# Self-attention's start: small loads issued by ScalarE, weight waits by block, the value weights' split moved

## What is computed

```python
x = _rmsnorm(tokens, norm_w)
q = x @ Wq
kv = x @ Wkv
k, v = jnp.split(kv, 2, axis=-1)
q = _head_rmsnorm(q, q_gamma)
k = _head_rmsnorm(k, k_gamma)
sim = jnp.einsum('bhid,bhjd->bhij', q, k)
sim = jnp.tanh(sim / SOFTCLAMP) * SOFTCLAMP
attn = jax.nn.softmax(sim * DIM_HEAD ** (-0.5), axis=-1)
out = jnp.einsum('bhij,bhjd->bhid', attn, v)
```

## Time and profile before

| | |
|---|---|
| median of 3 runs | 1844.41 us (1841.74 to 1845.32) |
| the profiled execution | 1844.2 us |
| its span (first to last instruction) | 1842.6 us |
| PE, DVE, ACT, POOL busy | 96%, 78%, 64%, 59% |
| granted TensorE clock, mean | 0.99 |

### The profile page before, as it was taken

One profiled execution on the slowest core, in us unless ns is written; L12 is line 12 of the kernel. 1 busy time (PEld: TensorE's weight loads), 2 busy tenths in 40 slices (PEclk: granted clock), 3 DMA queues, 4 the chain that ended last, 5 costly groups with the idle time before them and its releaser, 6 DMA issues.

```text
span 1842.6 us, 43008 instructions
## 1 busy us (share of the span) xinstructions
PE 1773.5 (96%) x14154; PEld 1481.7 (80%) x14154; DVE 1441.9 (78%) x3344; ACT 1170.6 (64%) x2674; POOL 1093.9 (59%) x1217
## 2 busy tenths in 40 slices
PE   5999999999997999999999999999999999989997
PEld 4777777777776899999999999899999999965443
DVE  5787789788887687777777788777777778788887
ACT  4876777765665466666566666656666656655664
POOL 3443445543344766866776755577878777552554
PEclk9999999999998999999999999999999999999999
DMA  4321323111113414414423433314322341551111
GB/s 157 109 74 64 117 75 111 41 50 30 40 50 104 156 48 149 129 60 133 129 91 105 142 104 94 110 48 120 93 73 82 93 113 47 129 118 50 57 62 63
DMA packets 109580, 166.89 MB, mean 91 GB/s; under 512 B 32488, under 2 KB 67672, under 8 KB 109512
## 3 DMA queue, kind: packets, MB, share of 16 engines
q1 hardware_dynamic: 91016, 129.77, 22.7%
q0 software_dynamic: 14656, 28.92, 5.7%
q10 hardware_dynamic: 3840, 7.34, 1.3%
HBM read 109.25 MB, written 50.46 MB: 87 GB/s over the span
## 4 chain that ended last, share of the span: by engine, by line
PE 58%; DVE 15%; issue 10%; POOL 7%; DMA 5%; ACT 4%; POOLq 1%; DVEq 0%; SPq 0%; ACTq 0%
PE att_ps_T L517 5%; PE att_ps_P L1648 5%; PE att_ps_SA L1672 4%; PE att_ps_P L1636 4%; PE att_ps_SB L579 4%; PE att_ps_P L1700 3%; PE att_ps_O L1636 3%; PE att_ps_T L1636 3%; PE att_ps_T L1648 2%; PE att_ps_P L1686 2%; DMA ca_ct<-ct_kept 2%; PE att_ps_O L1648 2%; PE att_ps_P L1711 2%; DMA out_dram<-ff_y_out 2%; PE att_ps_T L1700 2%
## 5 line engine op out<-in xcount | busy, mean ns | idle before, releaser
L1453 POOL TENSOR_TENSOR ca_pr<-ca_pr,ca_rec 112x750 f32<-112x750 f32 x256 | 366.8, 1453 | 182.8 <-DVE ca_rec L1932 179.8
L402 POOL TENSOR_TENSOR sa_p_lo<-sa_pr,sa_p_hi 112x448 fp32r<-112x448 f32 x128 | 147.2, 1162 | 255.2 <-ACT sa_p_hi L671 254.3
L1817 ACT ACTIVATE ca_big<-att_ps_P 126x384 fp32r<-126x384 f32 (+1 forms) x254 | 105.2, 449 | 65.1 <-PE att_ps_P L1686 63.1
L1811 ACT ACTIVATE ca_pr<-att_ps_SA,ca_nmax 112x750 f32<-112x750 f32 x128 | 113.7, 888 | 22.6 <-DVE ca_nmax L1928 12.2
L822 DVE RECIPROCAL sa_sums<-sa_sums 128x224 f32<-128x224 f32 x64 | 99.2, 1550 | 32.3 <-ACT sa_sums L680 31.8
L1937 DVE TENSOR_TENSOR ca_big<-att_ps_P,ca_big 126x384 fp32r<-126x384 f32 (+1 forms) x254 | 119.6, 498 | 5.5 <-ACT ca_big L1817 5.2
L1928 DVE TENSOR_REDUCE ca_nmax<-att_ps_SA 112x1 f32<-112x752 f32 x128 | 119.1, 930 | 0.1
L1928 DVE TENSOR_REDUCE ca_nmax<-att_ps_SB 112x1 f32<-112x752 f32 x128 | 119.0, 930 | 0.0
L1648 PE MATMUL att_ps_P<-ca_w_hi,ca_ct 128*126 128x256 f32 x570 | 116.5, 284 | 0.0
L1811 ACT ACTIVATE ca_pr<-att_ps_SB,ca_nmax 112x750 f32<-112x750 f32 x128 | 113.2, 885 | 0.1
L1686 PEld LDWEIGHTS att_ps_P<-att_ident,ca_pr 64*126 64x126 f32 (+1 forms) x1524 | 85.3, 138 | 13.7 <-issue 9.4
(11 more groups left out here) (344 smaller groups left out, 6659.1 us busy)
## 6 DMA issues: line engine op xcount, KB each, us to landing
ct_kept<-ca_ct SPq DMA_DIRECT2D x8, 1134.0 KB, 9.1
ca_ct<-ct_kept POOLq DMA_DIRECT2D x8, 1134.0 KB, 8.3
ct_kept<-ca_ct SPq DMA_DIRECT2D x8, 1116.0 KB, 11.5
ca_ct<-ct_kept POOLq DMA_DIRECT2D x8, 1116.0 KB, 10.4
sa_xin<-in_x_dram SPq DMA_DIRECT2D x16, 448.0 KB, 3.9
xt_kept<-ca_xt SPq DMA_DIRECT2D x8, 896.0 KB, 5.2
ca_xt<-xt_kept POOLq DMA_DIRECT2D x8, 896.0 KB, 5.1
ternary<-ca_stage SPq DMA_DIRECT2D x36, 172.0 KB, 1.9
```

The lines of the kernel that those rows point to most:

```text
L402: pool.tensor_tensor(p_lo[:, h % NB, :], pr[:, h % NB, :], f32(p_hi[:, h % NB, :]), ALU.subtract).then_inc(p_split, 1)
L1453: pool.tensor_tensor(w, w, rec[:, h % PB, c:c + 1].to_broadcast([R, S]), ALU.mult).then_inc(norm_done, 1)
L1811: act.activation(pr[:, h % PB, c, :].rearrange("r (a s) -> r a s", a=2), two_halves(psum[slot]), ACT.Exp, bias=nmax[:, h % PB, c:c + 1], a ...
L1817: act.activation(weights_view(h, c, x, False), blocks_view(source.bank, x), ACT.Copy).then_inc(t_hi_done, 1)
```

## The change

1. The three loads of constants are issued by ScalarE, ahead of its first instruction (and of the load of its function table), no longer by SyncE ahead of x.
2. `w_done` counts blocks of 128 rows: each of VectorE's L879 instructions increments it. All waits on it are multiplied by `KC` = 4. In the first batch TensorE waits inside `project`, before the first of a block's three passes, for that block alone.
3. The split of the value weights (piece 2) is moved: on ScalarE from behind the squares of `Q0` to behind those of `K0`, on VectorE from ahead of the reduction `HK0` to behind the scaling of `K0`.

```diff
     def sync(sp):
-        sp.dma_start(wnorm[:, :], norm_w.rearrange("(k p) -> p k", p=P), allow_slow_non_contiguous=True).then_inc(consts, 16)
-        for t, gamma in enumerate((q_gamma, k_gamma)):
-            sp.dma_start(gam[:, t, :], gamma.rearrange("(p t) d -> (t d) p", t=2),
-                         allow_slow_non_contiguous=True).then_inc(consts, 16)
...
                 elif n in (2, 3, 4):
-                    sp.wait_ge(w_done, n - 1)
+                    sp.wait_ge(w_done, KC * (n - 1))
...
-        def project(u, at):
+        def project(u, at, arriving=False):
...
             for n, (xs, ws, k) in enumerate(passes):
+                if arriving and n % 3 == 0:
+                    pe.wait_ge(w_done, KC * i + k + 1)
                 mm = pe.matmul(ps(u)[0:R, :], xs[:, k, c * R:c * R + R], ws[i][:, k, :],
...
-                        else:
-                            pe.wait_ge(w_done, 2 * batches[n][0] + WEIGHTS_FOR[name])
+                        elif batches[n][0]:
+                            pe.wait_ge(w_done, KC * (2 + WEIGHTS_FOR[name]))
...
+                    if isinstance(b, int) and b == -1 and n == 1:
+                        if name in WEIGHTS_FOR:
+                            project(name, batches[n][1], arriving=True)
+                            continue
...
-                    if name == "Q0" and isinstance(b, int) and g * B + b + n == 0:
+                    if name == "K0" and isinstance(b, int) and g * B + b + n == 0:
                         split_weights(2)
...
+        act.dma_start(wnorm[:, :], norm_w.rearrange("(k p) -> p k", p=P), allow_slow_non_contiguous=True).then_inc(consts, 16)
+        for t, gamma in enumerate((q_gamma, k_gamma)):
+            act.dma_start(gam[:, t, :], gamma.rearrange("(p t) d -> (t d) p", t=2),
+                         allow_slow_non_contiguous=True).then_inc(consts, 16)
...
-                lo = dve.scalar_tensor_tensor(w_lo[i][:, k, :], waiting(n)[:, k, :], wnorm[:, k:k + 1], f32(w_hi[i][:, k, :]), ALU.mult, ALU.subtract)
-            if k + 1 == KC:
-                lo.then_inc(w_done, 1)
+                dve.scalar_tensor_tensor(w_lo[i][:, k, :], waiting(n)[:, k, :], wnorm[:, k:k + 1], f32(w_hi[i][:, k, :]),
+                                         ALU.mult, ALU.subtract).then_inc(w_done, 1)
...
-                        elif name == "HK0":
-                            weights_lo(2)
                     do(name, batches[n][0], b, batches[n][1])
+                    if isinstance(b, int) and g * B + b + n == 0 and name == "K0":
+                        weights_lo(2)
```

More of the change, by code:

```diff
@@ L325, in load_weights @@
                 elif n == 7:
-                    sp.wait_ge(w_done, 4)
+                    sp.wait_ge(w_done, KC * 4)
                 sp.dma_start(waiting(n), blocks[i].rearrange("(k p) n -> p k n", p=P)).then_inc(w_in[n % 2], 16)
@@ L377, in sync @@
                     if b == B - 2:
-                        sp.wait_ge(w_done, 5)
+                        sp.wait_ge(w_done, KC * 5)
                     load_feed_forward(b, counter(b, g, B))
```

## The result

| | kernel before | changed kernel |
|---|---|---|
| median, 20 runs each | 1843.38 us (1839.74 to 1845.32) | 1846.06 us (1843.32 to 1849.53) |
| ratio | | 1.0015, 95% interval 1.0009 to 1.0021 |
| the profiled execution | 1844.2 us | 1844.55 us |
| its span | 1842.6 us | 1843.0 us |
| granted TensorE clock, mean | 0.99 | 0.991 |

A forecast was written before the change was run, and what follows sets the result against it. TensorE's own time was taken to bound the kernel behind the start, so only an earlier T0 could gain. Nothing gained at T0 (0.0) plus 0.5 for the clock on 1844.2 gave 1844.7 us, range 1840.8 to 1847.4.

The forecast's parts named there:

- if the four take 2.8: Sign that the prediction is wrong: the value weights' four low parts on VectorE take 2.8 us, not 6 to 7.
- Equal packets: Constants' loads beside large loads: a DMA engine passes one 4-byte packet per 2 KB packet, about 91 ns a pair.
- half of the 160 slip through before the large stream is dense: Constants' 160 packets per DMA engine: half pass before about 3.4 us; the other 80, paired with large ones, take 7.3 us.
- C: Time at which all constants have landed and VectorE can start: taken as 9.5 us, against 4.46 before the change.
- From C to HK0 and K1: Start of the kernel: Q0 2.55 us after the constants land, HK0 11.2 after them, K1 4.18 after HK0.
- alternation: Value weights' four low parts on VectorE take turns with GpSimd's split of Wo: 6.6 us instead of 2.8 alone.
- The first turn: First of VectorE's four value-weight low parts beside GpSimd: 1.55 us, the other three 1.69 each.
- no hold-up by GpSimd: Rival, chance 0.10: the moved split isn't slowed, HK1 at 28.75 with constants at 9.5, 1840.5 us in all.
- the forecast's case: Constants late and VectorE alternating with GpSimd: HK1 near 32.5, T0 near 37, 1844.7 us; chance 0.53.
- VectorE loses the turn: Rival, chance 0.10: each of the four low parts waits for two GpSimd instructions, HK1 at 34.4, 1849 us.
- The term of 0.5: TensorE's half-clock stretch reaching further after a longer idle before T0 (4.4 us, not 2.46): 0 to 1.6 more, taken as 0.5.

The follow-up runs named there:

- the second profile: The changed kernel run once more without an edit, for another profile: 1848.73 us (one run), the four low parts 5.63 us, T0 at 39.23.
- the third profile: The changed kernel again, unedited, on the chip of its GpSimd-waits partner: median 1846.25 us, ratio 1.0017 to the kernel before, T0 at 40.61.
- the key weights held back: Changed kernel, but SyncE loads the key weights only once the constants have landed: median 1841.14 us, ratio 0.9987 to the kernel before.
- late gammas: Changed kernel, but SyncE loads the norm weight ahead of x and the gammas behind the key weights: median 1838.45 us, ratio 0.9978 to before.

## Why the prediction was right, and where its steps were not

The median lies 1.4 us above the predicted one and inside the range, but two of the sum's terms were off by about 4 us each, with opposite signs in the profiled execution. That its T0 came out within 0.5 of the forecast is luck. By its own signs the prediction fails there: it was to be wrong "if the four take 2.8", and they took 2.73.

**When the constants land: right in kind, off by 4.** Equal packets hold (95 beside 96), and the first step to fail is "half of the 160 slip through before the large stream is dense". By 6 us 528 of the queue's 2608 packets had gone, a fifth and not half: the norm weight's 512, most of them in the gap from 4 to 5 us, and none or nearly none of the gammas'. The prediction read 86% of the engines for the small packets before as the pace of the beginning. From 3.0 to 3.5 a single small packet passed beside 93 large ones, where turns by packet would give some 93 as well, and from 4 to 5 only 385 passed on engines that were busy for less than half of the time. So the small queue itself was slow at the beginning, and why stays open. With C = 13.45 instead of 9.5 the edit costs 2.8 at Q0 and gains nothing.

**From C to HK0 and K1: right.** Q0 at C + 2.50 (predicted 2.55, though its three terms 0.66, 1.13 and 0.70 add up to 2.49), HK0 at C + 11.61 (11.2; TensorE's full clock came later in K0), K1 4.21 behind HK0 (4.18).

**The split: alternation is real, but it is one of two outcomes.** 6.6 us was predicted, and where the two engines alternate it takes 5.6 to 5.8. Beside GpSimd's low parts the turn was sized well: GpSimd's low parts in the second profile, whose own length is 1.26, came to 1.72 us (counted: 1.69) in the median of four:

```profile
L430 POOL TENSOR_TENSOR sa_w_lo<-sa_stage,sa_w_hi x4: 1257/1724/1735, 30.2 to 35.3; 128x512 fp32r<-128x512 f32 x4
```

The first turn was not: VectorE's first low part took 0.81 there and not 1.55. What I missed is that VectorE can keep the turn for all four in a row, at 2.73. The rows on which the hold-up rested show no meeting in which VectorE kept the turn over several instructions. The rival "no hold-up by GpSimd" was given 0.10 and is what the profiled execution shows; two other profiles of the same kernel show the forecast's case. "VectorE loses the turn" was in none.

**T0 and the sum.** The two errors nearly cancel in the profile: +4.0 at the constants, -3.9 at the split, T0 at 37.53 against the predicted 37. In the profile that was held up all the way from the same C, T0 is at 40.61, 3.5 behind the kernel before, and the execution 1847.8 us. The second and the third profile are the forecast's own case, constants late and turns alternating, and their executions (1848.7 and 1847.8) lie above the range. What keeps the median inside it, 2.7 and not 0.5 us above before, is that other runs lie lower, like the first profile's. The first profile also gained 1.6 from the clock in K1, against a kernel before that had the half-clock stretch there. So the sign of the median is due to the constants, whose own price, alone, is 4.7; the two other edits give about 2.5 back.

**The clock.** In the first profile no half-clock stretch came in K1 (1.00 from 28 to 32 us, where the earlier trace rows had 0.51), with 2.10 of idle before it. The idle time alone doesn't decide that: in the second profile it is 2.11, and the clock is 0.68. The stretches' rows (window, its length, PE, PEld, DVE, ACT, POOL busy, granted clock, DMA share, GB/s), of the first profile:

```profile
28.00:32.00 4.00, 2.73 (x12) 2.10 (x13) 3.90 (x9) 0.00 (x0) 4.00 (x3) 1.00 0.00 0
...
40.00:44.00 4.00, 4.00 (x27) 2.97 (x25) 0.77 (x2) 1.49 (x4) 1.72 (x2) 0.72 0.48 180
```

of the second:

```profile
28.00:32.00 4.00, 3.94 (x12) 2.93 (x13) 4.00 (x5) 0.00 (x0) 4.00 (x4) 0.68 0.00 0
...
48.00:52.00 4.00, 3.88 (x39) 3.18 (x34) 1.81 (x4) 3.97 (x11) 2.25 (x2) 0.74 0.59 140
```

and of the third, with 4.07 of idle ahead of T0:

```profile
40.00:44.00 4.00, 3.39 (x11) 2.65 (x12) 2.42 (x7) 0.69 (x2) 3.14 (x4) 0.50 0.69 266
```

The term of 0.5 was meant for an idle time over 4 us ahead of T0. From T0 to the next batch's transposes it takes 8.4 us in the kernel before, in the first profile (idle 2.47) and in the second (idle 3.81), and 9.15 in the third; with the key weights held back (idle 4.08) it takes 8.98. So the term is nothing in the first two and 0.5 to 0.7 where the idle time was over 4. With the block waits alone and with late gammas it takes 6.9, and no half-clock stretch falls between: one costs 1.6 there, as the prediction counted.

Behind the next batch's transposes it takes 1797.0 in the first profile, 1799.5 and 1796.4 in the two others. The second has a half-clock stretch more there (0.74 from 48 to 52 us, where the first has 1.00). None of my steps accounts for that.

**The rest.** x was used at 5.06, 0.5 earlier than forecast; nothing behind 46 us changed its length in the first pair of profiles; the later loads and GpSimd's scaling cost nothing.

## What to carry to other kernels

Moving small element-wise loads to a second queue didn't take them out of the way of the large ones here; from 6 us on each of their packets went behind a large one until the large ones ran out. Issue what is needed first in the first queue, and what is needed late behind the large loads. Where VectorE and GpSimd work on SBUF operands side by side, look at more than one profile before you trust a duration, and order the two by a semaphore if the one is on the path and the other isn't.

## What the runs showed of the hardware

- From 6 to 12 us two hardware queues passed 4-byte and 2 KB packets in nearly equal numbers, 1193 and 1124, where the small ones alone reach 1253 in 0.5 us. Up to 6 us they did not (1 small beside 93 large, 385 beside 28, 21 beside 152), and why stays open. A gamma's 4 KB took 11.4 us from issue to landing beside x, Wq and the key weights, where it took 2.4 ahead of them in the kernel before.
- The same four VectorE instructions took 2.73 us or 5.58 to 5.84 beside GpSimd. In the first case one GpSimd instruction took nearly 4 us, in the second several took up to 1.75 each. In eight profiles the point in GpSimd's current instruction went with which it was: up to 0.34 us in, VectorE kept the turn for all four; from 0.59 on, it didn't. In the kernel before, one VectorE instruction waited at 0.27, so this is no general rule.
- Little is enough to turn one outcome into the other. The first and the third profile of the changed kernel have the first low part at 29.73 and 29.70, and GpSimd's first instruction at 25.68 and 25.86: 0.18 us between them, and T0 3 us apart.
